# Expert results: scattered with an add into one zeroed row per token, in place of two written regions added on the way back

## What is computed

```python
logits = xn @ router_w
probs = jax.nn.softmax(logits, axis=-1)
topv, topi = jax.lax.top_k(probs, K)
topv = topv / jnp.sum(topv, axis=-1, keepdims=True)
comb = jnp.sum(jax.nn.one_hot(topi, E, dtype=xn.dtype) * topv[..., None], axis=1)
out = jnp.zeros_like(xf)
for e in range(E):
    out = out + comb[:, e:e + 1] * _swiglu(xn, gate_up_w[e], down_w[e])
out = out + _swiglu(xn, shared_gate_up_w, shared_down_w)
```

## Time and profile before

| | |
|---|---|
| time, median of 3 runs | 5952.53 us (5944.75 to 5954.58) |
| profiled execution | 5925.85 us, span 5923.6 us |
| TensorE busy | 4948.8 us, 84% of the span |
| VectorE busy | 4153.3 us, 70% |
| GpSimd busy | 3297.0 us, 56% |
| ScalarE busy | 3100.1 us, 52% |
| indirect DMAs to `results` | 312, 302.1 us of GpSimd |
| indirect DMAs to `pairs` | 256, 255.5 us of GpSimd |
| read backs of `results` | 32 of 512 KB, median 4.6 us to landing |

### The profile page before, as it was taken

How to read it: one execution, slowest core, us unless ns; L and a number is a source line. 1 busy time by engine, 2 the same in 40 slices (tenths; PEclk the granted TensorE clock), 3 DMA queues, 4 the chain that set the end, 5 groups by cost and what they waited for, 6 DMA issues and landing times. The chain is left out here.

```text
span 5923.6 us, 79232 instructions
## 1 busy us (share of the span) xinstructions
PE 4948.8 (84%) x22446; PEld 2500.9 (42%) x22446; DVE 4153.3 (70%) x6070; ACT 3100.1 (52%) x5312; POOL 3297.0 (56%) x2373
## 2 busy tenths in 40 slices
PE   5888889889887788977787999855997899964997
PEld 1333333333333443434343555433664344432664
DVE  5999999999997573057665878743775566642775
ACT  5666666666664464235554777621332577821332
POOL 3888988898895363025443444345333555526333
PEclk8999999999999899999888999977997999976998
DMA  2244322222221002000003333112553433311555
GB/s 81 90 137 151 118 87 89 88 87 90 83 90 47 0 0 87 0 0 0 6 6 83 87 85 93 36 50 75 188 188 107 105 94 97 77 38 55 181 188 171
DMA packets 203028, 494.17 MB, mean 83 GB/s; under 512 B 32432, under 2 KB 57520, under 8 KB 191280
## 3 DMA queue, kind: packets, MB, share of 16 engines
q1 hardware_dynamic: 183536, 451.33, 24.5%
q0 software_dynamic: 18176, 37.79, 1.9%
q10 hardware_dynamic: 960, 0.79, 0.1%
HBM read 381.65 MB, written 108.12 MB: 83 GB/s over the span
## 5 line engine op out<-in xcount | busy, mean ns | idle before, releaser
L396 POOL TENSOR_TENSOR mamba_bu<-mamba_du,mamba_b_all 128x1024 f32<-128x1024 f32 x512 | 1198.7, 2357 | 185.7 <-PE psum L490 170.1
L667 DVE TENSOR_TENSOR_SCAN mamba_bu<-psum,mamba_bu 128x512 f32<-128x512 f32 x1024 | 1190.0, 1206 | 69.2 <-ACT psum L599 34.4
L490 PE MATMUL psum<-mamba_bu,consts 128*128 128x512 f32 x2048 | 965.3, 594 | 0.0
L599 ACT ACTIVATE psum<-mamba_delta,A 128x510 f32<-128x510 f32 x1024 | 682.9, 683 | 387.8 <-DVE mamba_bu L667 374.6
L1764 ACT ACTIVATE ffn_moe_act<-ffn_moe_act 128x512 f32<-128x512 f32 x344 | 216.9, 631 | 721.5 <-DVE ffn_moe_act L1808 721.4
L1649 POOL DMA_INDIRECT results<-ffn_moe_y_rows,ffn_moe_row_of x312 | 302.1, 968 | 507.7 <-DVE ffn_moe_y_rows L1839 426.8
L673 DVE TENSOR_TENSOR mamba_bu<-mamba_bu,psum 128x1024 f32<-128x1024 f32 x448 | 537.1, 1199 | 5.2 <-PE psum L475 3.0
L490 PEld LDWEIGHTS psum<-mamba_bu,consts 128*128 128x128 f32 x2048 | 392.5, 192 | 345.7 <-issue 327.4
L2204 POOL TENSOR_TENSOR loc_q_bd<-loc_q_max,weights_l1a 128x512 fp32r<-128x512 f32 x256 | 274.8, 1103 | 381.0 <-DVE loc_q_max L2459 372.2
L2204 POOL TENSOR_TENSOR cau_q_bd<-cau_q_max,weights_l1b 128x512 fp32r<-128x512 f32 x256 | 258.4, 1043 | 243.2 <-DVE cau_q_max L2459 177.5
L2450 DVE TENSOR_REDUCE cau_top<-psum 128x2 f32<-128x512 f32 (+1 forms) x384 | 263.2, 692 | 182.5 <-PE psum L2274 168.7
(11 more groups left out here) (413 smaller groups left out, 11064.0 us busy)
## 6 DMA issues: line engine op xcount, KB each, us to landing
mamba_b_all<-b_rows SPq DMA_DIRECT2D x256, 512.0 KB, 4.3
ffn_moe_w_gu<-gate_up_parts SPq DMA_DIRECT2D x78, 1024.0 KB
pairs<-empty_rows SPq DMA_DIRECT2D x6, 3432.0 KB, 13.1
ffn_moe_got<-pairs SPq DMA_DIRECT2D x78, 264.0 KB, 3.2
ffn_moe_w_down<-in_l_moe SPq DMA_DIRECT2D x78, 256.0 KB
mamba_c_rows<-b_rows SPq DMA_DIRECT2D x32, 512.0 KB
qk_rows<-loc_qk SPq DMA_DIRECT2D x16, 1024.0 KB, 8.6
ffn_moe_back<-results SPq DMA_DIRECT2D x32, 512.0 KB, 4.6
```

The lines of the kernel that those rows point to most:

```text
L396: nc.gpsimd.tensor_tensor(bu[:, J % BU, :, :], du[:, q % 2, :, :], b, ALU.mult).then_inc(bu_ready, 1)
L490: last = nc.tensor.matmul(ysum[:, h, :], mem.ident, bu[:, J % BU, h, :], start=False, stop=(n == NST - 1), skip_group_check=True)
L599: nc.scalar.activation(by_seq(dA[i % DECAYS])[:, :, 1:S], by_seq(delta[:, q % 2, h, :])[:, :, 1:S], ACT.Exp, scale=mem.A[:, q % 2, h * NST ...
L667: nc.vector.tensor_tensor_scan(bu[:, J % BU, h, :], dA[i % DECAYS], bu[:, J % BU, h, :], 0.0, ALU.mult, ALU.add).then_inc(scanned, 1)
```

## The change

There is one region of 8192 rows (and the spare rows). It is zeroed at the start of each stage: VectorE fills `y_rows[:, 0]` with zeros (semaphore `cleared`), and SyncE writes it 16 times to `results` ahead of the first weights (`zeroed`). The row number no longer depends on the rank. The scatters carry `compute_op=ALU.add`, so each reads its destination rows, adds, and writes them. Since the two choices of a token lie in different blocks, GpSimd waits before block b's four scatters until block b-1's have landed (before the first block, for the zeros). VectorE's first `scale_y` also waits for the zeros, since it overwrites their source. The read back takes 256 KB per tile, and the adds on GpSimd and VectorE are gone; TensorE waits for the landing itself.

```diff
-        back = sb("back", RING, 2, QUART * D)
+        back = sb("back", RING, QUART * D)
...
+            sp.wait_ge(cleared, 1 + LEAD)
+            by_place = results[0:TOK, :].rearrange("(p j) c -> p (j c)", p=128)
+            for t in range(NT):
+                sp.dma_start(by_place[:, t * QUART * D:(t + 1) * QUART * D], y_rows[:, 0, :, :].rearrange("p s d -> p (s d)")).then_inc(zeroed, 16)
             for b in range(HELD):
                 load_weights_of(b)
...
-            of_rank = results[0:2 * TOK, :].rearrange("(k p j) c -> p k (j c)", k=2, p=128)
             for t in range(NT):
                 if t >= RING:
                     sp.wait_ge(turned_back, t - RING + 1 + LEAD)
-                sp.dma_start(back[:, t % RING, :, :], of_rank[:, :, t * QUART * D:(t + 1) * QUART * D]).then_inc(back_landed[t % RING], 16)
+                sp.dma_start(back[:, t % RING, :], by_place[:, t * QUART * D:(t + 1) * QUART * D]).then_inc(back_landed[t % RING], 16)
...
                 pool.wait_ge(y_rows_ready, b + 1 + LEAD)
                 pool.sem_inc(PASSED[0], 1)
+                if b == 0:
+                    pool.wait_ge(zeroed, 16 * NT + LEAD)
+                else:
+                    pool.wait_ge(y_stored[(b - 1) % RING], 16 * QUART * ((b - 1) // RING + 1))
+                pool.sem_inc(PASSED[0], 1)
                 for s in range(QUART):
                     nc.gpsimd.indirect_dma_start(results, bass.IndirectOffsetOnAxis(row_of[:, b % RING, s:s + 1], 0),
-                                                 y_rows[:, b % RING, s, :], None).then_inc(y_stored[b % RING], 16)
-            for t in range(0, NT, 2):
-                pool.wait_ge(back_landed[t % RING], 16 * (t // RING + 1) + LEAD)
-                pool.sem_inc(PASSED[0], 1)
-                nc.gpsimd.tensor_tensor(back[:, t % RING, 0, :], back[:, t % RING, 0, :], back[:, t % RING, 1, :], ALU.add).then_inc(even_added, 1)
+                                                 y_rows[:, b % RING, s, :], None, compute_op=ALU.add).then_inc(y_stored[b % RING], 16)
...
-                pe.wait_ge(odd_added if t % 2 else even_added, t // 2 + 1 + LEAD)
+                pe.wait_ge(back_landed[t % RING], 16 * (t // RING + 1) + LEAD)
...
-                nc.vector.scalar_tensor_tensor(row_of[:, r, :], other[:, h, :], float(TOK), column(3), ALU.mult, ALU.add).then_inc(marked, 1)
+                nc.vector.tensor_scalar(row_of[:, r, :], column(3), 1.0, None, ALU.mult).then_inc(marked, 1)
...
             def scale_y(b):
                 dve.wait_ge(y_turned, b + 1 + LEAD)
+                if b == 0:
+                    dve.wait_ge(zeroed, 16 * NT + LEAD)
...
             for t in range(SENT):
                 send_meta(t)
+            nc.vector.memset(y_rows[:, 0, :, :], 0.0).then_inc(cleared, 1)
...
             for t in range(NT):
-                if t % 2 == 1:
-                    dve.wait_ge(back_landed[t % RING], 16 * (t // RING + 1) + LEAD)
-                    nc.vector.tensor_tensor(back[:, t % RING, 0, :], back[:, t % RING, 0, :], back[:, t % RING, 1, :], ALU.add).then_inc(odd_added, 1)
-                if t >= 1:
-                    add_back(t - 1)
-            add_back(NT - 1)
+                add_back(t)
```

More of the change, by code:

```diff
@@ L1546, in l1_experts @@
         (rows_turned, rows_sent_ready, meta_ready, x_high, x_ready, gate_ready, clipped, silu_ready, up_ready, hidden_ready, down_done,
-         shared_added, block_turned, marked, y_ready, y_turned, y_rows_ready, even_added, odd_added, turned_back, added, in_dram
+         shared_added, block_turned, marked, y_ready, y_turned, y_rows_ready, cleared, zeroed, turned_back, added, in_dram
          ) = ctx.enter_context(signals(
              nc, stage, "rows_turned", "rows_sent", "meta", "x_high", "x", "gate", "clipped", "silu", "up", "hidden", "down",
-             "shared_added", "block_turned", "marked", "y", "y_turned", "y_rows", "even_added", "odd_added", "turned_back", "added", "in_dram"))
+             "shared_added", "block_turned", "marked", "y", "y_turned", "y_rows", "cleared", "zeroed", "turned_back", "added", "in_dram"))
         scattered = ctx.enter_context(from_zero(nc, stage + "_scattered", *"0123"))
@@ L1738, in _ @@
             for t in range(NT):
-                pe.wait_ge(odd_added if t % 2 else even_added, t // 2 + 1 + LEAD)
+                pe.wait_ge(back_landed[t % RING], 16 * (t // RING + 1) + LEAD)
                 pe.wait_ge(added, t - 1 + LEAD)
                 for s in range(QUART):
-                    last = nc.tensor.transpose(mem.bank[t % 2][:, s * 128:(s + 1) * 128], back[:, t % RING, 0, s * D:(s + 1) * D], mem.ident)
+                    last = nc.tensor.transpose(mem.bank[t % 2][:, s * 128:(s + 1) * 128], back[:, t % RING, s * D:(s + 1) * D], mem.ident)
                 last.then_inc(turned_back, 1)
@@ L3144 @@
         "qk": nc.dram_tensor("qk_rows", (2, 4, 128, T), F32).ap(),
-        "results": nc.dram_tensor("results", (2 * TOK + RING * BLK, D), F32).ap(),
+        "results": nc.dram_tensor("results", (TOK + RING * BLK, D), F32).ap(),
         "gate_up": nc.dram_tensor("gate_up_parts", (NE, D, 2 * GU), F32).ap(),
```

## The result

The change makes the kernel slower: 6029.02 us, median of four runs (6027.75 to 6034.56), against 5952.75 us for the kernel before (5944.75 to 5954.58). The ratio is 1.0135, 95% interval 1.0122 to 1.0147: 76 us lost where 15.5 were to be gained. 6029.02 lies just above the range (5924 to 6025). The profiled execution took 6028.98 us.

A forecast was written before the change was run, and what follows sets the result against it. TensorE was taken to bound the blocks, GpSimd the sending, a chain of waits the read back. Read backs gain 24.7, tails lose 9.2: 15.5 us gained, 5937.0 against 5952.53, range 5924 to 6025.

The forecast's parts named there:

- the term X: Block scatters: four times an issue's growth plus a landing's growth from adding; 1.4 us a block, ends 0 and 6.1.
- the cover of 2.3: Block stretch: the new wait ends 2.3 us before the wait already there, so adding costs nothing below that.
- The landing beside the loads: Block scatters: 2.9 us today beside weight loads; adding was taken to lengthen it by 1.0, about half a read.
- The issue term: Block scatters on GpSimd: each adding issue grows by 0.1 us from 0.97, 0.4 for a block's four.
- The upper bound, doubling: Block scatters: an adding scatter issued as two, 0.97 us more per issue.
- the slower rival: Blocks: waiting on the previous block's landing sets the pace; at X = 2.9, 36 us slower, 5989; chance 0.30.
- The tail: End of the blocks, no cover: the last block's scatters finish later, 1.8 + 2 x 1.4 a stage, 9.2 us in all.
- The read back: Results read after the blocks: halved reads and no add save 12.0 us in stage one, 12.7 in stage two.
- The "same" rival: Read back: landings stay at 4.3 and 5.7 us whatever the size; gain 10.0 less 9.2, 5952; chance 0.18.
- The zeroing: Sending stretch: sixteen 256 KB writes ahead of the first weights cost zero; as a rival, 28 us slower, chance 0.02.
- The clock: Block stretch: TensorE's granted clock below 0.98 was listed as a sign that the forecast is wrong.
- its low end: Range's fast end: X = 0 and reads landing 0.7 us sooner in ten rounds and two starts; 28.8 gained, 5924.

The follow-up runs named there:

- the run with long issues: Changed kernel with plain scatters in place of adding ones, each followed on GpSimd by a memset to lengthen the issue, wait kept: 5931.39 us, ratio 0.9971.
- the loads small: Changed kernel with weight loads after the first three blocks cut to 16 columns of each weight, adding scatters and wait kept: 5939.27 us, ratio 0.9986.
- the loads are held: Changed kernel with block b+3's 1024 KB weight load also waiting until block b-1's scatters have landed: 5936.31 us, ratio 0.9975.

## Why the prediction was wrong

**The step that failed** is the term X, what the adding form costs a block, "X = 0.4 + 1.0 = 1.4", and in it the issue. An issue grew by 1.556 - 0.969 = 0.59, four times 2.3, where 0.4 was taken: that alone uses up the cover of 2.3. The landing beside the loads went from the 2.9 it was counted from to 4.8 (median of the 71 waits that a landing ended), of which 0.6 is the issue again, so 1.3 more, where 1.0 was taken. X is 3.6. The issue term was the larger error: 0.1 was read from the earlier trace rows, where 512 and 528 bytes cost the same. Those rows vary the row's size and hold the form fixed, and no row of them has an adding scatter. The upper bound, doubling, was the nearer end. An estimate from the Trainium skill's rule, three descriptors for two ("DMA: Bandwidth & Descriptors", section "SWDGE vs HWDGE vs iDMA", and "Collectives: The Full Stack", section "The bandwidth ceiling: the fold count and why AG ≠ RS ≠ AR"), put it at 1.45; 1.556 is 1.61 times the plain issue, and so this case's runs are nearer to that rule than to my figure.

**The cover was sized wrongly too.** 2.9 is the median over all four scatters of a block, but the wait hangs on the fourth. In the kernel before the fourth lands after 3.45 us (median of both stages; 2.25 in the last blocks, where no load is left), so the cover was 1.8 and not 2.3. Counted from there the landing grew by 4.8 - 3.45 - 0.6 = 0.8 and X is 3.1; either way the excess is 1.3 a block. And the growth beside the loads is not the form's own: the run with long issues has plain landings of 4.5 to 5.2 us in the same order. The longer issues push the last scatter against the next load, and the load stretches its landing. With the loads small or held the fourth lands after 3.3, X is 4 x 0.59 + (3.3 - 2.25 - 0.6) = 2.8, and the loop, 5.59 + 3.3 + 0.8 = 9.7, stays under 9.86.

**The mechanism of the slower rival was right**, with its kind of decision: an X over the cover is paid in every block. The median spacing went from 9.85 to 11.14 and 11.18, 1.3 a block. Its X of 2.9 was near the 3.1, but its excess of 0.6 leaned on a cover of 2.3. The range ended at 6025, which the text put to an X of 3.4 or so and thus an excess of 1.1; the measured excess is 1.3. Neither case of the text foresaw that the loads' place in the block would move. What the runs show is that the wait on the block before and the adding form together cost the time, and the loads' place with them; how much of the form's part is its longer issue and how much its landing is not settled, as the run with long issues was 0.5 us short of the adding span.

**The tail.** Predicted 1.8 + 2X = 4.6 a stage. Measured in stage one: the last block follows after 9.63 in place of 5.09 (4.5), its four issues take 1.8 more, and the read starts 3.34 in place of 2.33 behind the last issue (1.0): 7.3. It is 1.8 + 2 x 2.8 = 7.4, as the formula has it with the X of landings without loads. It stays where the loads are held, and is most of the 9.5 us by which that run's blocks of stage one are above before.

**The read back** came out: 27.0 and 32.0 were predicted, 24.5 and 30.1 measured. The line of the reads in the change:

```profile
L1627 SPq DMA_DIRECT2D ffn_moe_back<-results x32: 319/320/430, 4571.8 to 6012.8; - x32
...
DMA to landing us min/median/max: 2.6/3.0/5.9
```

By stage the medians are 2.9 and 3.6, against the 3.2 and 4.2 taken. The "same" rival, a landing that stays at 4.3 and 5.7, is out.

**The zeroing** at nothing was right: run again, the kernel before sends no faster. **The clock** was not part of it: 1.00 was granted from 4160 to 4495 in the change and in the kernel before alike. **The base** deserved more care: 5925.85 was taken with "it was 27 under the median", and the same gain was carried over, which was sound; but a stage table made from it alone blames the sending for 23 us that are not the change's.

Put together from what was measured against the kernel before, run again: 27.0 gained in the read back, some 15 lost in the tails, 37 x 2 x 1.27 = 94 in the other blocks, 82 us slower; the medians are 76 apart. One slip of the prediction is small: at its low end, ten rounds and two starts of 0.7 are 8.4 and not 7.7.

## What to carry to other kernels

A wait of an engine on its own DMA's landing turns a queue into a loop: issue times plus landing plus wake-up. Compare that loop with the bottleneck's period, and take for the landing that of the last link, not the median of all, and as it is with a big transfer beside it. Look at which big transfer starts there; moving that transfer by half a block was worth some 90 us here, 6029.02 and 5936.31 with 5952.75 and 5949.07 for the kernel before beside them. Price a new form of an instruction from a row where the same thing changes, or weigh the bounds; a row that varies something else is no evidence. And take a second profile of the kernel before, before a stage is blamed.

## What was not expected of the hardware

- An adding indirect scatter of 128 rows of 512 B costs GpSimd 1.556 us to issue (1.550 to 1.607), a plain one 0.969.
- It makes about 143 packets where the plain one makes 32. In the change from 4160 to 4495 us, with 120 scatters:

```profile
q0 software_dynamic: 17104, 7.79, 22.7%
```

The recorded bytes are the same 64 KB each, but a scatter takes 0.227 x 335 / 120 = 0.63 us of all 16 engines, against 0.18.
- The landing of a block's last adding scatter takes 3.3 us without a large load beside it and 4.8 (median of 71, at most 6.7) in the change. A plain one takes 2.25 without, 3.45 in the kernel before, and 3.5 to 5.2 in the 14 waits that it ended beside loads in the run with long issues. So the load stretches both forms. That the adding form's many small packets stand between the load's is possible by the counts and was not tested by itself.
- The issue of the next scatter starts 0.77 us after the landing that it waited for.
